# Edge network: one addition per group of four tiles, from sums at register offsets

## The reference

```
alpha = concat(K[dst] * K[src], K[dst] * (edge @ Ke[h])) * scale
gate  = sigmoid(ln(alpha) * g + b)
m     = (concat(V[src], edge @ Ve[h]) @ Wu[h] + bu[h]) * gate
m     = leaky(ln(m @ Wm[h] + bm[h]) * mg + mb)
head  = segment_sum(m, dst, num_segments=6250)
```

## Time and profile before

| | us |
|---|---|
| median of 3 runs | 13353.01 (13352.68 to 13353.71) |
| span of the profiled execution | 13346.2 |
| sweep over the edges, first gather to last affine step | 4131 to 11274 |

### The profile page before, as it was taken

How to read it: one execution, slowest core, us unless ns; L and a number is a source line. 1 busy time by engine, 2 the same in 40 slices (tenths; PEclk the granted TensorE clock), 3 DMA queues, 4 the chain that set the end, 5 groups by cost and what they waited for, 6 DMA issues and landing times.

```text
span 13346.2 us, 181640 instructions
## 1 busy us (share of the span) xinstructions
PE 9273.5 (69%) x45190; PEld 6132.3 (46%) x45190; DVE 9007.8 (67%) x20368; ACT 5821.3 (44%) x11467; POOL 9313.9 (70%) x6569
## 2 busy tenths in 40 slices
PE   1344444444475888888888888888888887779886
PEld 0233333333224665666666666665666565333222
DVE  3233333333207888888888888888888887157996
ACT  0111111111003666666666666666666665026332
POOL 1688888888504888888888888888888885000553
PEclk9999999999997999999999999989999998989997
DMA  9766666666783333333343333333334333869553
GB/s 412 233 159 149 152 152 151 153 149 152 198 360 123 120 119 120 119 119 120 119 119 119 120 119 119 120 119 120 119 119 120 119 119 97 347 260 330 177 186 104
DMA packets 1232552, 2147.34 MB, mean 161 GB/s; under 512 B 345985, under 2 KB 768210, under 8 KB 1218579
## 3 DMA queue, kind: packets, MB, share of 16 engines
q1 hardware_dynamic: 838120, 1657.69, 36.0%
q0 software_dynamic: 390240, 484.27, 16.5%
q10 hardware_dynamic: 4048, 3.51, 0.1%
HBM read 1652.11 MB, written 492.84 MB: 161 GB/s over the span
## 4 chain that ended last, share of the span: by engine, by line
POOL 41%; issue 23%; PE 11%; DVE 8%; DMA 8%; ACT 4%; SPq 3%; DVEq 1%; POOLq 1%; another core or an unknown queue 0%; ACTq 0%; PEldq 0%
POOL arena L1367 21%; POOL adj L1406 13%; POOL arena L1419 5%; DMA arena<-adj 4%; SPq L1471 3%; PE psum L1278 2%; DMA adj<-put_val,put_idx 2%; ACT arena L984 2%; POOL arena L1422 2%; PE psum L1201 1%; PE psum L1136 1%; DVE arena L901 1%; PE psum L1290 1%; PE psum L1214 1%; PE psum L1191 1%
## 5 line engine op out<-in xcount | busy, mean ns | idle before, releaser
L1406 POOL DMA_INDIRECT adj<-put_val,put_idx x1616 | 2639.9, 1634 | 832.4 <-issue 461.0
L984 ACT ACTIVATE arena<-arena 128x128 f32<-128x128 f32 x6464 | 2657.2, 488 | 296.2 <-DVE arena L775 111.5
L1115 PE MATMUL psum<-ke,arena 64*128 64x256 f32 x3232 | 1451.5, 640 | 1871.3 <-DMA arena<-in_edge_t 1871.3
L1367 POOL DMA_INDIRECT arena<-table1q,idx_dst x1616 | 2255.6, 1396 | 492.4 <-issue 492.4
L1367 POOL DMA_INDIRECT arena<-table,idx_blk x1616 | 1898.1, 1175 | 432.2 <-issue 376.2
L1115 PEld LDWEIGHTS psum<-ke,arena 64*128 64x128 f32 x3232 | 1041.2, 330 | 2281.2 <-issue 2013.9
L1201 PEld LDWEIGHTS psum<-wm,arena 128*128 128x128 f32 x12928 | 1751.3, 203 | 608.0 <-issue 509.3
L990 ACT ACTIVATE arena<-psum,cols 128x512 f32<-128x512 f32 x1616 | 1248.4, 773 | 1717.6 <-PE psum L1183 1382.5
L1191 PE MATMUL psum<-arena,wvu 128*128 128x512 f32 x3232 | 1890.9, 670 | 84.6 <-DVE arena L704 59.1
L1214 PE MATMUL psum<-arena 128*128 128x128 f32 x6464 | 1116.7, 325 | 1118.3 <-DVE arena L731 1104.4
L1201 PE MATMUL psum<-wm,arena 128*128 128x64 f32 x12928 | 1793.8, 285 | 5.9 <-issue 4.6
(11 more groups left out here) (210 smaller groups left out, 12378.0 us busy)
## 6 DMA issues: line engine op xcount, KB each, us to landing
arena<-adj SPq DMA_DIRECT2D x192, 1568.0 KB, 12.5
arena<-adj SPq DMA_DIRECT2D x336, 896.0 KB, 4.7
kept_keys<-arena SPq DMA_DIRECT2D x404, 512.0 KB
arena<-kept_keys SPq DMA_DIRECT2D x404, 512.0 KB
adj<-arena SPq DMA_DIRECT2D x98, 1568.0 KB
arena<-in_edge_t SPq DMA_DIRECT2D x808, 128.0 KB
kept_hot<-arena SPq DMA_DIRECT2D x404, 256.0 KB
arena<-kept_hot SPq DMA_DIRECT2D x404, 256.0 KB
```

The source lines that it names most:

```text
L984: A.activation(to, at_, ACT.Identity, bias=shift[z][:, n:n + 1], scale=rstd[z][:, n:n + 1]).then_inc(normed, 1)
L1115: last = M.matmul(psum[:, 2 + 2 * z + j, t * H * D:(t + 1) * H * D], edge0[z][:, 2 * j + t, :], ke[D:P, :], start=True, stop=True)
L1367: K.indirect_dma_start(out=dst[:, t, :], out_offset=None, in_=table, in_offset=bass.IndirectOffsetOnAxis(ap=idx[:, t:t + 1], axis=0)).then ...
L1406: K.indirect_dma_start(out=adj, out_offset=bass.IndirectOffsetOnAxis(ap=put_idx[s][:, j:j + 1], axis=0), in_=put_val[s][:, j:j + 1], in_of ...
```

## The change

Four things are done otherwise.

- The four tiles of a group are summed into banks 0 and 1 (two heads in each), each tile at the column offset of its window from the first tile's window. TensorE reads these offsets (0 to 384) into registers, 16 per four groups (`block_offsets`). They are computed once by VectorE into the first row of `rel`, whose contents are no longer needed.
- Both banks are first opened with zeros by a bf16 product of a zero row with a repeated zero (`clear_sums`), since the windows overlap and differ.
- VectorE makes one addition of 2 x 512 columns per group at the first tile's base, at the end of its step. It loads four bases per four groups instead of 16. `added1` now counts groups. `acc` has three windows more at its end, and the three small rows for the bias are kept there before the sweep.
- The mixing bias is put into bank 6 by one product of 512 columns per two tiles, ahead of the mixing products instead of behind them, and `bm_parts` holds the bias twice. The transposes of `turn_x` go to bank 7.

```diff
-NW = NP + WIN
+NW = NP + G * WIN
-        bm_parts = sb("bm_parts", [3, H * D], BF16)
+        zero_row = sb("zero_row", [1, P], BF16)
+        bm_parts = sb("bm_parts", [3, 2 * H * D], BF16)
+        offs = rel[0:1, :].bitcast(I32)
-        def block_bases(engine, g):
-            return bases(engine, dst_t[0:1, bass.ds(g * G, U * G)])
+        def group_bases(engine, g):
+            first = dst_t[0:1, bass.ds(g * G, U * G)].rearrange("p (u t) -> p u t", t=G)[:, :, 0]
+            return bases(engine, first)
+        def block_offsets(engine, g):
+            _, regs = nc.values_load_multi_w_load_instructions(
+                offs[0:1, bass.ds(g * G, U * G)], engines=(engine,), min_val=0, max_val=(G - 1) * WIN, ...)
+            return regs
...
 VectorE
-            def add_tile(added, g, t, at_, sums):
-                after(dve, added, g * G + t)
-                V.tensor_tensor(at_, at_, sums, ALU.add).then_inc(added, 1)
+            link(V.tensor_tensor(offs..., dst_t..., dst_t[... 0:1].to_broadcast([1, NG, G]), ALU.subtract))
-                def add(t):
-                    if now[4]:
-                        dve.wait_ge(sums1, 2 * (i - 4) + t // 2 + 1)
-                        add_tile(added1, i - 4, t, acc[:, :, bass.ds(regs[t], WIN)], ...)
+                def add():
+                    dve.wait_ge(sums1, 2 * (i - 3))
+                    after(dve, added1, i - 4)
+                    own = acc[:, :, bass.ds(held[s], G * WIN)]
+                    V.tensor_tensor(own, own, psum[:, 0:2, :], ALU.add).then_inc(added1, 1)
-                add(0)
-                add(1)
                 if now[1]:
                     gate_m(3)
-                add(2)
-                add(3)
+                if now[4]:
+                    add()
...
 TensorE
+                if now[4] and s == 0:
+                    held[:] = block_offsets(PE, i - 4)
                 def o_pair(j):
-                    pe.wait_ge(gm_ready, H * (i - 1))
                     after(pe, o_taken, 2 * (i - 2) + j)
+                    M.matmul(psum[:, 6, :], ones3[:, :], bm_parts[:, :], start=True, stop=False)
+                    pe.wait_ge(gm_ready, H * (i - 1))
...
-                        last = M.matmul(psum[:, 6, at_:at_ + H * D], ones3[:, :], bm_parts[:, :],
-                                        start=False, stop=True)
+                def clear_sums():
+                    after(pe, added1, i - 4)
+                    for half in range(2):
+                        M.matmul(psum[:, half, :], zero_row[0:1, :], zero_row[0:1, 0:1].to_broadcast([1, G * WIN]),
+                                 start=True, stop=False)
                 def sums(j):
-                    after(pe, added1, G * (i - 5) + 2 * j + 2)
                     for t in (2 * j, 2 * j + 1):
                         for half in range(2):
-                            last = M.matmul(psum[:, 1 + 6 * j, at_:at_ + WIN], msg..., onehot[z][:, t, :], start=True, stop=True)
+                            last = M.matmul(psum[:, half, bass.ds(held[G * s + t], WIN)], msg..., onehot[z][:, t, :],
+                                            start=False, stop=t == G - 1)
                 if now[4]:
+                    clear_sums()
                     sums(0)
```

More of the change, by code:

```diff
@@ L141, in gnn @@
         vecs = sb("vecs", [D, 6])
-        bm_row = sb("bm_row", [1, H, D])
-        bm_rest = sb("bm_rest", [1, H, D])
-        bm_up = sb("bm_up", [1, H, D])
+        bm_row, bm_rest, bm_up = (acc[0:1, i // 2, NP + i % 2 * H * D:NP + (i % 2 + 1) * H * D].rearrange(
+            "p (h d) -> p h d", h=H) for i in range(3))
+        zero_row = sb("zero_row", [1, P], BF16)
         bm_part = [sb(f"bm_part{i}", [1, H * D], BF16) for i in range(3)]
-        bm_parts = sb("bm_parts", [3, H * D], BF16)
+        bm_parts = sb("bm_parts", [3, 2 * H * D], BF16)
         ones3 = sb("ones3", [3, P], BF16)
@@ L418, in halves_of @@
             return slice(half * HALF + i * CH_N, half * HALF + (i + 1) * CH_N)
-        def block_bases(engine, g):
-            return bases(engine, dst_t[0:1, bass.ds(g * G, U * G)])
+        def group_bases(engine, g):
[3 more added lines that the diff above has]
+            _, regs = nc.values_load_multi_w_load_instructions(
+                offs[0:1, bass.ds(g * G, U * G)], engines=(engine,), min_val=0, max_val=(G - 1) * WIN,
+                skip_runtime_bounds_check_because="every node has an edge, so a tile begins at most a window on")
+            return regs
         @block.vector
@@ L692, in sweep1 @@
                 if now[4] and s == 0:
-                    held[:] = block_bases(DVE, i - 4)
-                regs = held[G * s:G * s + G]
+                    held[:] = group_bases(DVE, i - 4)
                 def stats(t):
@@ L947, in _ @@
             for i in range(3):
-                A.dma_start(bm_parts[i:i + 1, :], bm_part[i][:, :]).then_inc(bm_in, 16)
+                for t in range(2):
+                    A.dma_start(bm_parts[i:i + 1, t * H * D:(t + 1) * H * D], bm_part[i][:, :]).then_inc(bm_in, 16)
             dve_done(f"key_turn{len(TC) - 1}")
@@ L1006, in sweep1 @@
                     after(act, m_done, H * (i - 3))
-                    A.activation(xt[s][0:D].rearrange("p t n -> p (t n)"), psum[0:D, 0, :],
+                    A.activation(xt[s][0:D].rearrange("p t n -> p (t n)"), psum[0:D, 7, :],
                                  ACT.Copy).then_inc(xt_ready, 1)
@@ L1175, in turn_x @@
                     for t in range(G):
-                        last = M.transpose(psum[0:D, 0, t * P:(t + 1) * P], pair[s][:, t, 0:D], ident[:, :])
+                        last = M.transpose(psum[0:D, 7, t * P:(t + 1) * P], pair[s][:, t, 0:D], ident[:, :])
                     last.then_inc(xt_turned, 1)
@@ L1194, in o_pair @@
                 def o_pair(j):
+                    after(pe, o_taken, 2 * (i - 2) + j)
+                    M.matmul(psum[:, 6, :], ones3[:, :], bm_parts[:, :], start=True, stop=False)
                     pe.wait_ge(gm_ready, H * (i - 1))
-                    after(pe, o_taken, 2 * (i - 2) + j)
                     for t in range(2):
@@ L1209, in sums @@
                     pe.wait_ge(msg_ready, i - 3)
-                    after(pe, added1, G * (i - 5) + 2 * j + 2)
                     for t in (2 * j, 2 * j + 1):
                         for half in range(2):
-                            at_ = (t % 2 * 2 + half) * WIN
-                            last = M.matmul(psum[:, 1 + 6 * j, at_:at_ + WIN],
+                            last = M.matmul(psum[:, half, bass.ds(held[G * s + t], WIN)],
                                             msg[z][:, t * H + 2 * half:t * H + 2 * half + 2, :].rearrange("p h d -> p (h d)"),
-                                            onehot[z][:, t, :], start=True, stop=True)
+                                            onehot[z][:, t, :], start=False, stop=t == G - 1)
                     last.then_inc(sums1, 1)
@@ L1240, in sweep1 @@
                     sums(1)
+            held = []
             steps(pe, sweep1, NG, 8, 4)
-            pe.wait_ge(added1, T)
+            pe.wait_ge(added1, NG)
             for i in range(NBLK):
```

17 lines of the change are left out of this document (9 added, 8 removed).

## The result

The changed kernel takes 13389.4 us in the median (13370.5 to 13435.8, 12 runs) against 13354.9 of the kernel before on the same chip (13349.5 to 13368.4, 12 runs): ratio 1.0025, 95% interval 1.0017 to 1.0034. It is slower by 34.5 us, where I had forecast 13341 and gave "slower" 0.12. The range, 13320 to 13400, holds the time; the direction is wrong. Profiled span: 13388.3.

A forecast was written before the change was run, and what follows sets the result against it. A loop of VectorE and GpSimd, 17.51 us a group, was taken as the bound, with the additions outside it. -14 us in the loop and +1.8 outside gave -12 on 13346.2; with 6.8 carried along, 13341, range 13320 to 13400.

The forecast's parts named there:

- "slower": Whole kernel: the third and fourth rivals together, a time above the 27 us that count as no change; chance 0.12.
- The addition: VectorE, end of each group's step: one 128x1024 addition from PSUM at 1.25 us replaces four at 418 ns.
- the clearing and bias products: TensorE, each group: two clearing and two bias products of 512 columns at 0.42 us each, +0.84 us a group.
- The passes at register offsets: TensorE's sums: 16 passes a group with PSUM addresses from registers, 0.05 us each, 0.8 us a group.
- Rivals 2 and 3: Rival 2: VectorE bounds, all its savings count, 13122, chance 0.06. Rival 3: register offsets break TensorE's overlap, 13960, chance 0.09.
- The register load: VectorE, once per four groups: loading four values instead of 16 takes 0.5 us instead of 1.11.
- The gain that was forecast: Start of VectorE's messages (L731) in every fourth group: lateness shrinks by 0.14 us, 101 times, 14 us.
- the 0.14 us in the fourth group: VectorE's messages start 0.16 us behind GpSimd's affine step because of the register load; this was to shrink to 0.02.
- the loop of 17.51 us: VectorE's messages to long product L683, held gather, three more gathers, GpSimd's affine steps: the group's period, without the additions.
- rival 4: TensorE's grown loop body no longer stays on the chip: 1 us per four groups, 101 us, 13440; chance 0.03.
- the bias: TensorE, each group: four products of 256 columns at 0.21 us replaced by two of 512 at 0.42 us.

The follow-up runs named there:

- a32_bias_old: Changed kernel with the mixing bias as before (four products of 256 columns behind the mixing products) and VectorE's loop moved by 32 instructions: 13370.5 us, ratio 1.0009.
- shift96: Changed kernel with 96 semaphore increments more ahead of VectorE's loop, which moves its code: 13317.0 us, ratio 0.9975 to the kernel before.
- a32: Whole changed kernel, new bias too, with VectorE's loop moved by 32 instructions: 13304.3 us, ratio 0.9971 to the kernel before.
- after: The changed kernel itself, with all parts of the change and its code not moved: 13389.4 us, ratio 1.0025 to the kernel before.
- before_shift94: Kernel before with 94 semaphore increments more ahead of VectorE's loop, which moves its code: 13366.5 us, ratio 1.0013.
- shift64: Changed kernel with 64 semaphore increments more ahead of VectorE's loop, nothing changed inside it: 13312.0 us, ratio 0.9971 to the kernel before.
- before_bias: Kernel before with the new bias alone, one product of 512 columns per two tiles ahead of the mixing products: 13325.5 us, ratio 0.9974.

## Why the prediction was wrong

**The parts were priced about right.** The addition takes 1.212 us (forecast 1.25), the clearing and bias products 0.42 each (0.42), and doubling the clearing changes nothing. The passes at register offsets keep their pace, eight in 1.15 us where the earlier trace rows has 1.16, and 325 ns a pass in a32_bias_old as in the earlier trace rows. So the 0.8 us I gave them is nearer to nothing:

```profile
7026.01 1.15 PE L1225 MATMUL psum<-arena 128*128 128x128 f32 x8
```

Rivals 2 and 3 did not come. (Two slips of arithmetic in the prediction bear on nothing: 8 passes in 1.16 us are 0.145 a step, not 0.13, and 404 x 1.5 is 606.) The register load was mis-sized, 0.96 us against 0.5; without the fetch it costs nothing even so, since it runs under the addition in front of it (idle time ahead of the statistics 14.3 us in shift96, 120.0 in the earlier trace rows).

**The gain that was forecast does not exist.** The prediction read the 0.14 us in the fourth group as VectorE's work that comes too late. It is the register step behind the wait, and the change puts it into two groups of four instead of one: +10 us where -14 stood. The additions part by itself measured +0.09%, "no change".

**Step that failed: the loop of 17.51 us was taken as fixed.** The prediction lets the start of L731 act on the period in one way only, later is longer. The table above has 0.3 to 0.8 us late at 16.88 and 3 to 5 us late at 18.27. The mean period of its columns is 17.565 before, 17.590 for a32_bias_old, 17.457 for a32, 17.641 for after. Times 404 groups, the differences to before are +10, -44 and +31 us; the ratios times 13355 are +12, -39 and +33. So nearly all of each difference lies in these periods. The table sorts the groups and does not foretell them: at 1.5 to 3 us late the mean period is 17.53 in after and 17.00 in before_shift94.

**Second step that failed: rival 4 was put on TensorE alone, at 0.03.** The row told that nothing is fetched before; I asked only whose body grows. VectorE's shrinks, and that moved it: from a place where it touches three blocks to one where it touches four. Without the fetch the changed kernel stands at 0.9971 to 0.9975 (a32, shift64, shift96), with it at 1.0025: +0.5%, 72 us, by the ratios of a32 and after. With the bias ahead, this is what turns a gain into a loss.

**Third: the bias was priced for TensorE's columns only.** In order of the edits, by the ratios: additions +12 us, the bias ahead -51 (1.0009 to 0.9971), the fetch +72; sum +33, of 34.5 measured. The terms hold only in this order. The bias ahead alone is -35 in the kernel before, and with the fetch present it turns round: 1.0025 with it, 0.9974 without, +68 us. The fetch is +17 in the kernel before and -47 with the old bias (1.0009 to 0.9974). Each moves messages between the rows of the table, into the one that gains or into those that lose; that this alone makes the size of each term was not tested.

Shown: the fetch is there or not by the place of the code, and moving it away gives back the loss (shift64, a32, shift96); a message that starts first holds the gather, and one that starts just behind it does not, which gives 1.5% in the kernel before, 2.2% on a32_bias_old and 1.7% on a32. Open: why the order of the bias lowers TensorE's granted clock; it goes with longer stretches at 1.2 GHz (share of the window 0.185 before, 0.229 in before_bias, 0.230 in a32, 0.262 after; 0.18 in a32_bias_old), but no run holds the clock fixed.

## What to carry to other kernels

Where two engines share a port, ask of each pair of starts who comes first: a wait "as early as possible" can hold the partner of the loop for longer than it gains, and here starting one engine a tenth of a microsecond behind the other was worth more than the whole change. Look at the instruction queue before and after any edit to a body in a hardware loop, on each engine, shrunk ones too; if one appears, move the loop by some dozens of instructions before judging the edit. And time the parts of a change singly and together: the bias ahead was worth -51 us without the fetch and +68 with it.

## What the hardware showed beside this

- A loop of 280 instructions fetched five packets of 8 KB a round, with 2.86 us between the last operation of a round and the next, and 1.06 us more behind the first statistic. The same loop 32, 64 or 96 instructions further back fetched none and had 0.0 to 0.1 us there; 128 further back it fetched again.
- A gather of GpSimd took 1.0 us, and 1.8 us or more where the message on VectorE, with two SBUF inputs, had started more than 0.05 us ahead of it.
- A wait carried by a register step of VectorE's sequencer let the next operation start 0.13 us behind what it waited for, and 0.03 where the operation carried the wait.
- A load of four values that lie four apart takes 0.96 us, 16 in a row 1.11.
- A fp32 addition of 128x1024 with one input in PSUM takes 1.212 us, four of 128x256 took 4 x 0.418.
